# A gated cross-attention and feed-forward block in float32 on one core: a second x1 buffer, four ffn buffers, a reordered start and a reordered last tile

## What is computed

```
query = einsum('bnc,dc->bnd', ctx, Wq) + bq        # ctx: (4, 512, 256), d = 128
key   = einsum('bnc,dc->bnd', ctx, Wk) + bk
attention = softmax(einsum('bnd,bmd->bnm', query, key))
x = x + tanh(g_xattn) * einsum('bln,bmn->blm', layernorm(x), attention)
z = normalise(layernorm(x)) * ln_weight + ln_bias
x = x + tanh(g_ffn) * (einsum('bsk,ok->bso', z, sign(weight)) * max|weight| * gamma + beta)
```

## Time and profile before

| | us |
|---|---|
| median of 3 runs | 133.01 (132.58 to 133.08) |
| the profiled execution, its own time | 132.29 |
| its span, from the first to the last instruction | 130.8 |
| PE busy | 119.5 (91% of the span) |
| DVE busy | 94.8 (73%) |
| POOL busy | 92.3 (71%) |
| ACT busy | 86.8 (66%) |
| mean granted clock of PE | 0.977 of full |

### The profile page before, as it was taken

One profiled execution on the slowest core, in us unless ns is written; L12 is line 12 of the kernel. 1 busy time (PEld: TensorE's weight loads), 2 busy tenths in 40 slices (PEclk: granted clock), 3 DMA queues, 4 the chain that ended last, 5 costly groups with the idle time before them and its releaser, 6 DMA issues.

```text
span 130.8 us, 1869 instructions
## 1 busy us (share of the span) xinstructions
PE 119.5 (91%) x558; PEld 94.7 (72%) x558; DVE 94.8 (73%) x187; ACT 86.8 (66%) x185; POOL 92.3 (71%) x106
## 2 busy tenths in 40 slices
PE   5968999999999999948999999999999999999830
PEld 4517688888888878826888888878888888887730
DVE  1148699897988992479764992898859738997672
ACT  4243999999998889037797797179997940334300
POOL 3006899916329989998363799994649999839790
PEclk9999999999999999996899999999999999999996
DMA  3949999735532500247450502357000202220043
GB/s 80 246 141 393 392 388 296 306 76 152 186 89 74 160 0 5 83 147 250 165 160 0 160 0 85 116 205 228 13 3 3 74 11 80 80 80 0 0 182 139
DMA packets 10649, 17.15 MB, mean 131 GB/s; under 512 B 1808, under 2 KB 2576, under 8 KB 10640
## 3 DMA queue, kind: packets, MB, share of 16 engines
q1 hardware_dynamic: 9920, 17.04, 38.3%
q10 hardware_dynamic: 720, 0.00, 0.3%
HBM read 12.59 MB, written 4.19 MB: 128 GB/s over the span
## 4 chain that ended last, share of the span: by engine, by line
PE 53%; ACT 17%; POOL 14%; DVE 6%; issue 4%; POOLq 1%; ACTq 1%; DVEq 1%
PE ps_y L372 23%; PE ps_ffn L385 14%; POOL x L863 5%; PE ps_turn L339 4%; PE ps_score L332 4%; ACT prob L507 3%; PE ps_ffn L310 3%; POOL x L868 3%; PE ps_score L446 3%; ACT prob L513 2%; ACT k_hi L496 2%; POOL xt_lo L851 2%; ACT x_sb L544 2%; ACT q_hi L496 1%; DVE neg_max L640 1%
## 5 line engine op out<-in xcount | busy, mean ns | idle before, releaser
L863 POOL TENSOR_TENSOR x<-x,shift 128x512 f32<-128x512 f32 x16 | 21.1, 1320 | 8.1 <-ACT unread L538 8.1
L851 POOL TENSOR_TENSOR xt_lo<-xt_raw,xt_hi 128x512 fp32r<-128x512 f32 x16 | 21.6, 1350 | 7.3 <-ACT xt_hi L519 4.2
L685 DVE SCALAR_TENSOR_TENSOR zw<-x,neg_mean,ln_w 128x512 f32<-128x512 f32 x16 | 19.4, 1209 | 0.4
L868 POOL TENSOR_TENSOR x<-x,ffn 128x512 f32<-128x512 f32 x14 | 18.9, 1356 | 0.0
L372 PE MATMUL ps_y<-pt_hi,xt_hi 128*128 128x512 f32 x64 | 18.9, 418 | 0.0
L507 ACT ACTIVATE prob<-ps_score,neg_max 128x512 f32<-128x512 f32 x14 | 9.5, 681 | 13.8 <-DVE neg_max L640 13.8
L372 PE MATMUL ps_y<-pt_hi,xt_lo 128*128 128x512 f32 x64 | 18.4, 411 | 0.0
L555 ACT ACTIVATE zt_hi<-ps_turn 128x512 fp32r<-128x512 f32 x16 | 9.5, 594 | 12.9 <-PE ps_turn L339 12.9
L711 DVE SCALAR_TENSOR_TENSOR ffn<-ps_ffn,rstd,gain 128x512 f32<-128x512 f32 x15 | 11.2, 746 | 9.1 <-POOL x L868 4.1
L385 PE MATMUL ps_ffn<-w_sign,zt_hi 128*128 128x512 f32 x60 | 17.2, 408 | 0.5 <-DVE ffn L711 0.5
L372 PE MATMUL ps_y<-pt_lo,xt_hi 128*128 128x512 f32 x64 | 17.6, 396 | 0.0
(11 more groups left out here) (160 smaller groups left out, 241.5 us busy)
## 6 DMA issues: line engine op xcount, KB each, us to landing
xt_raw<-in_x_t_dram SPq DMA_DIRECT2D x16, 256.0 KB, 3.0
out_dram<-x SPq DMA_DIRECT2D x15, 256.0 KB, 2.0
ctx_sb<-in_ctx_t_dram SPq DMA_DIRECT2D x8, 256.0 KB, 6.8
x_sb<-in_x_dram SPq DMA_DIRECT2D x8, 256.0 KB, 5.0
ctx_sb<-in_x_dram SPq DMA_DIRECT2D x8, 256.0 KB, 6.2
w_raw<-in_weight_t_dram SPq DMA_DIRECT2D x4, 256.0 KB, 8.2
ln_w<-in_ln_weight_dram SPq DMA_DIRECT2D x1, 256.0 KB, 7.6
gain<-in_gamma_dram SPq DMA_DIRECT2D x1, 256.0 KB, 8.6
```

Source lines behind the costliest of these rows:

```text
L685: nc.vector.scalar_tensor_tensor(out=zw[:, t, :], in0=x1[:, t, :], scalar=neg_mean2[:, t:t + 1], in1=ln_w[:, :], op0=ALU.add, op1=ALU.mult)\
L851: nc.gpsimd.tensor_tensor(xt_lo[:, t, :, :], xt_raw[:, t, :, :], xt_hi[:, t, :, :].bitcast(f32), ALU.subtract).then_inc(xt_lo_done, 1)
L863: nc.gpsimd.tensor_tensor(x1[:, t, :], x1[:, t, :], shift[:, :], ALU.add).then_inc(x1b_done, 1)
L868: nc.gpsimd.tensor_tensor(x1[:, t, :], x1[:, t, :], ffn[:, t % 2, :], ALU.add)\
```

## The change

- `x1` gets a second buffer for the odd batches, in the place of the contexts of batches 2 and 3. `add_y` waits for a store only from batch 2 on, and then for that of two batches earlier.
- `ffn` has four buffers. `scale_ffn` waits for `add_ffn` of the same tile of the batch before.
- At the start the keys of batch 0 are projected first, then the queries in two halves of 256 columns, the second half into another bank (`ps_y[1]`); the first two `scores` need the first half alone. The query of batch 1 is projected with split operands, as all others were.
- The key weights are loaded by ACT's queue, ahead of the biases, and all three ahead of ACT's table load.
- On POOL `add_ffn(b, 0)` stands behind `power2(b, 1)` and `split_xt(b + 1, 1)`.
- In `last`, `power2(b, 0)` and `add_shift(b, 3)` stand earlier on POOL, the squares earlier on ACT, and DVE finishes each half of the last tile before it begins the other.
- On DVE two splits of batch 2's projection stand earlier.

The diff, cut to its core (declarations of semaphores and the places where only `x1` became `x1_buf[b % 2]` are left out):

```diff
-        ffn = sb("ffn", [P, 3, N])
+        ffn = sb("ffn", [P, T, N])
...
-        out_stored = [sem(f"out_stored{t}") for t in range(T)]
+        out_stored = [[sem(f"out_stored{i}_{t}") for t in range(T)] for i in range(2)]
...
+        x1_buf = (x1, ctx_sb[:, 2:4, :, :].rearrange("p b k l -> p (b k) l"))
...
+        q_first = ((ps_ffn[0], slice(0, L // 2), proj_ready), (ps_y[1], slice(L // 2, L), q_rest_ready))
...
-            for t in range(T):
-                sp.sem_inc(out_stored[t], 16)
+                sp.dma_start(out[b, t * P:(t + 1) * P, :], x1_buf[b % 2][:, t, :]).then_inc(out_stored[b % 2][t], 16)
+
+            load_ctx(0)
             sp.dma_start(wq_sb[:, :, :], wq_t.rearrange("(k p) d -> p k d", p=P)).then_inc(wq_in, 16)
-            load_ctx(0)
-            sp.dma_start(wk_sb[:, :, :], wk_t.rearrange("(k p) d -> p k d", p=P)).then_inc(wk_in, 16)
             load_ctx(1)
...
-                if b == 0 or (b, j) == (1, 0):
-
-                    for k in range(KC):
-                        if j == 0:
-                            pe.wait_ge(ctx_in[b][k], 16)
-                        mm = pe.matmul(bank[:, :], (wq_sb, wk_sb)[j][:, k, :], ctx_sb[:, b, k, :],
-                                       start=(k == 0), stop=(k == KC - 1))
-                    mm.then_inc(proj_ready, 1)
-                    return
...
+            def project_k0():
+
+                pe.wait_ge(wk_in, 16)
+                for k in range(KC):
+                    pe.wait_ge(ctx_in[0][k], 16)
+                    mm = pe.matmul(ps_ffn[1][:, :], wk_sb[:, k, :], ctx_sb[:, 0, k, :],
+                                   start=(k == 0), stop=(k == KC - 1))
+                mm.then_inc(proj_ready, 1)
+
+            def project_q0():
+
+                pe.wait_ge(wq_in, 16)
+                for bank, cols, ready in q_first:
+                    for k in range(KC):
+                        mm = pe.matmul(bank[:, cols], wq_sb[:, k, :], ctx_sb[:, 0, k, cols],
+                                       start=(k == 0), stop=(k == KC - 1))
+                    mm.then_inc(ready, 1)
+
             def scores(b, t):
+                if b == 0 and t == HALF:
+                    pe.wait_ge(q_rest_lo, 1)
                 if t == 0:
                     pe.wait_ge(proj_lo, 2 * (b + 1))
...
-            pe.wait_ge(wq_in, 16)
-            project(0, 0)
-            pe.wait_ge(wk_in, 16)
-            project(0, 1)
+            project_k0()
+            project_q0()
...
+            act.dma_start(wk_sb[:, :, :], wk_t.rearrange("(k p) d -> p k d", p=P)).then_inc(wk_in, 16)
+            act.dma_start(bqk[:, 1:2], bk.rearrange("(p a) -> p a", a=1)).then_inc(bias_in, 16)
+            act.dma_start(bqk[:, 0:1], bq.rearrange("(p a) -> p a", a=1)).then_inc(bias_in, 16)
             act.wait_ge(half_done, 1)
-
             nc.scalar.activation(table_in[:, :], neg_half[:, :], ACT.Tanh).then_inc(table_done, 1)
             act.wait_ge(table_done, 1)
-            act.dma_start(bqk[:, 0:1], bq.rearrange("(p a) -> p a", a=1)).then_inc(bias_in, 16)
-            act.dma_start(bqk[:, 1:2], bk.rearrange("(p a) -> p a", a=1)).then_inc(bias_in, 16)
...
-            for arrived, w, hi in ((wq_in, wq_sb, wq_hi), (wk_in, wk_sb, wk_hi)):
+            def round_k0():
+                act.wait_ge(proj_ready, 1)
+                nc.scalar.activation(k_hi[:, 0, :], ps_ffn[1][:, :], ACT.Identity,
+                                     bias=bqk[:, 1:2]).then_inc(proj_hi, 1)
+
+            def round_q0():
+                for (bank, cols, _), ready, count, done in zip(q_first, (proj_ready, q_rest_ready), (2, 1),
+                                                               (proj_hi, q_rest_hi)):
+                    act.wait_ge(ready, count)
+                    nc.scalar.activation(q_hi[:, 0, cols], bank[:, cols], ACT.Identity,
+                                         bias=bqk[:, 0:1]).then_inc(done, 1)
+
+            for arrived, w, hi in ((wk_in, wk_sb, wk_hi), (wq_in, wq_sb, wq_hi)):
                 act.wait_ge(arrived, 16)
                 nc.scalar.activation(hi[:, :, :], w[:, :, :], ACT.Copy).then_inc(w_hi_done, 1)
             act.wait_ge(bias_in, 16 * 2)
-            round_qk(0, 0)
-            round_qk(0, 1)
+            round_k0()
+            round_q0()
...
-            for t in range(T):
-                turned_ffn_hi(B - 1, t)
-                square_x1(B - 1, t)
+            square_x1(B - 1, 0)
+            square_x1(B - 1, 1)
+            turned_ffn_hi(B - 1, 0)
+            square_x1(B - 1, 2)
+            turned_ffn_hi(B - 1, 1)
+            square_x1(B - 1, 3)
+            turned_ffn_hi(B - 1, 2)
+            turned_ffn_hi(B - 1, 3)
...
-                dve.wait_ge(out_stored[t], 16 * (b + 1))
+                if b >= 2:
+                    dve.wait_ge(out_stored[b % 2][t], 16 * (b // 2))
                 dve.wait_ge(x_biased, T * b + t + 1)
                 dve.wait_ge(y_ready, T * b + t + 1)
-                nc.vector.scalar_tensor_tensor(out=x1[:, t, :], in0=ps_y[t % 2][:, :],
+                nc.vector.scalar_tensor_tensor(out=x1_buf[b % 2][:, t, :], in0=ps_y[t % 2][:, :],
...
-                if t >= 2:
-                    dve.wait_ge(out_done, T * b + t - 1)
-                nc.vector.scalar_tensor_tensor(out=ffn[:, t % 2, :], in0=ps_ffn[(t + 1) % 2][:, :],
+                if b > 0:
+                    dve.wait_ge(out_done, T * (b - 1) + t + 1)
+                nc.vector.scalar_tensor_tensor(out=ffn[:, t, :], in0=ps_ffn[(t + 1) % 2][:, :],
                                                scalar=rstd2[:, t:t + 1], in1=gain[:, :],
...
                 t = T - 1
+                dve.wait_ge(x1b_done, T * b + t + 1)
                 for h, cols in enumerate(halves):
                     dve.wait_ge(ffn_ready, 1 + T * b + t + 1 + h)
-                    nc.vector.scalar_tensor_tensor(out=ffn[:, 2, cols], in0=half_bank[h][:, cols],
+                    nc.vector.scalar_tensor_tensor(out=ffn[:, t, cols], in0=half_bank[h][:, cols],
                                                    scalar=rstd2[:, t:t + 1], in1=gain[:, cols],
                                                    op0=ALU.mult, op1=ALU.mult).then_inc(ffn_evac, 1)
-                dve.wait_ge(x1b_done, T * b + t + 1)
-                for h, cols in enumerate(halves):
                     dve.wait_ge(ffn_evac, 1 + T * b + t + 1 + h)
-                    nc.vector.tensor_tensor(x1[:, t, cols], x1[:, t, cols], ffn[:, 2, cols], ALU.add)\
+                    nc.vector.tensor_tensor(x1_buf[b % 2][:, t, cols], x1_buf[b % 2][:, t, cols], ffn[:, t, cols], ALU.add)\
                              .then_inc(last_out_done, 1)
...
-            for j, (w, hi, lo) in enumerate(((wq_sb, wq_hi, wq_lo), (wk_sb, wk_hi, wk_lo))):
+            for j, (w, hi, lo) in enumerate(((wk_sb, wk_hi, wk_lo), (wq_sb, wq_hi, wq_lo))):
                 dve.wait_ge(w_hi_done, j + 1)
                 nc.vector.tensor_tensor(lo[:, :, :], w[:, :, :], hi[:, :, :].bitcast(f32), ALU.subtract)\
                          .then_inc(w_lo_done, 1)
             dve.wait_ge(bias_in, 16 * 2)
-            rest_qk(0, 0)
-            rest_qk(0, 1)
+            dve.wait_ge(proj_hi, 1)
+            nc.vector.scalar_tensor_tensor(out=k_lo[:, 0, :], in0=ps_ffn[1][:, :], scalar=bqk[:, 1:2],
+                                           in1=k_hi[:, 0, :].bitcast(f32), op0=ALU.add, op1=ALU.subtract)\
+                     .then_inc(proj_lo, 1)
+            for (bank, cols, _), ready, count, done in zip(q_first, (proj_hi, q_rest_hi), (2, 1),
+                                                           (proj_lo, q_rest_lo)):
+                dve.wait_ge(ready, count)
+                nc.vector.scalar_tensor_tensor(out=q_lo[:, 0, cols], in0=bank[:, cols], scalar=bqk[:, 0:1],
+                                               in1=q_hi[:, 0, cols].bitcast(f32), op0=ALU.add,
+                                               op1=ALU.subtract).then_inc(done, 1)
...
+            rest_qk(2, 0)
             stats_x(0, (3,))
-            rest_qk(2, 0)
+            rest_qk(2, 1)
             weight_max(0)
-            rest_qk(2, 1)
...
-                add_ffn(b, 0)
                 power2(b, 1)
                 split_xt(b + 1, 1)
+                add_ffn(b, 0)
...
                 add_shift(b, 0)
+                power2(b, 0)
                 add_shift(b, 1)
-                power2(b, 0)
                 add_shift(b, 2)
                 power2(b, 1)
+                add_shift(b, 3)
                 add_ffn(b, 0)
                 add_ffn(b, 1)
-                add_shift(b, 3)
 
             nc.gpsimd.memset(neg_half[:, :], -0.5).then_inc(half_done, 1)
             nc.gpsimd.memset(q_hi[:, B - 1, :].bitcast(f32), 0.0).then_inc(later_zeroed, 1)
```

21 lines of the change are left out of this document (12 added, 9 removed).

## The result

| | before | after |
|---|---|---|
| median of the runs, us | 132.80 (132.05 to 133.08, 4 runs) | 124.38 (124.30 to 124.74, 4 runs) |
| ratio, 95% interval | | 0.938 (0.9335 to 0.9425) |
| profiled execution | 132.29 | 124.74 |
| its span | 130.8 | 122.8 |

Measured twice more, the same kernel took 125.12 us (124.95 to 125.35) and 124.78 us (124.09 to 125.55). So the runs shown first were on the lucky side, by about half a us (in their profile the clock came to full 1.1 us earlier than in the two later ones); even 125.12 lies just under the range, which ends at 125.2.

The account below looks back on a forecast made before the run. PE was taken to bound the steady state, ACT and PE the start, and short waits the end. Terms -0.5, -3.9 and -1.8 sum to -6.2 us: 126.1 profiled, 126.8 as median with 0.7 added; range 125.2 to 129.1.

Parts of the forecast that it names:

- The middle, -3.9: Batch 1's stretch on PE falls from 29.00 to 25.07 us: 2.3 of idleness and 1.6 of low clock.
- It costs nothing, its removal gives 0: DVE's 4.6 us of waits for stores, removed by the second `x1` buffer, were covered by PE's own work: 0.
- the moved `add_ffn` delays only a store, for which nothing waits: POOL's new order in batch 0's second half keeps the same sum of work and harms nothing.
- The rival in which the stall moves into batch 1: POOL's backlog makes `zw` or `xt_lo` late by up to 2 us; only the clock's 1.6 gained, 129.1 us; 16%.
- The clock's 1.6 us: Part of the middle's gain: PE's clock no longer falls to one half after its idleness for `zw`, 1.6 us.
- The start, -0.5: First stage: ACT's stream gains 0.25 us and PE 0.28 more; bounds 0 and -1.6.
- the hole closes: PE's 1.56 us of idleness for `k_lo` before the first `scores` goes, as keys are split during the queries' product.
- So ACT's stream of 27 us gains what the landing gains ... I take the middle, -0.25: ACT, without slack, gains only from contexts landing earlier, by one SP issue of half a us; 0.25 taken.
- The start comes whole: Rival: contexts land a us or more earlier and ACT's stream moves with PE's, 125.5 us; 10%.
- The end, -1.8: Behind PE's last feeds: last DVE addition at 126.5 instead of 128.26 us; bounds -0.9 and -2.3.
- The waits of 0.54 and 0.37: At the end, PE's wait for `scale_ffn` of tile 0 and the last additions' for `add_shift` of tile 3 go.
- 0.75 + 0.87 for tile 2: DVE's time for tile 2 at the end, within 3.5 us from PE's last full feed to the last addition.

Follow-up runs that it names:

- wk_sp_bias_late: Changed kernel with key weights back on SP's queue ahead of the contexts and biases back behind ACT's table load: 125.42 us, ratio to before 0.949.
- start_old: Changed kernel with its whole old start put back (loads, keys, queries, splits of batch 2): 126.49 us, kernel before 132.28.
- end_order: Changed kernel with the first half of the last tile scaled ahead of tile 2's addition on DVE: 123.94 us, run again 124.20.
- end_tile0: Changed kernel with the addition of the last batch's tile 0 on DVE instead of POOL: 125.04 us, kernel before 132.64.
- end_both: Changed kernel with the last tile's first half scaled ahead of tile 2's addition, and tile 0's addition moved to DVE: 125.49 us.
- ffn2: Changed kernel with two `ffn` buffers in batches 0 to 2, POOL's new order and two `x1` buffers kept: 127.37 us, kernel before 132.13.
- ffn2_pool_old: Changed kernel with two `ffn` buffers in batches 0 to 2 and POOL's old order, two `x1` buffers kept: 127.24 us, kernel before 131.33.
- x1_one: Changed kernel with a single `x1` buffer, four `ffn` buffers and POOL's new order kept: 127.07 us, kernel before 131.33.

## Why the prediction was right and wrong

**The middle, -3.9, was right in sum (4.04) and wrong in who earned it.** DVE's first wait (1.6 forecast, 1.65), the scaling of tile 3 behind `ffn_ready`, `zw` ahead of PE by about 1 us: all as worked out. Wrong was "It costs nothing, its removal gives 0", said of the second `x1` buffer, and "the moved `add_ffn` delays only a store, for which nothing waits". Nothing waits for it because of that buffer; without it DVE waits 3.71 us. The waits of the earlier trace rows were judged where they lay in the kernel before, behind a longer one, and not once that one was gone. POOL's new order, credited with part of the gain, gives nothing. The rival in which the stall moves into batch 1 didn't happen: POOL was busy 23.17 of 24.96 us there, and PE had no hole.

**The clock's 1.6 us is an amount for one profile.** Of the 38 runs of the kernel before that ran beside the experiments, 28 have a mean clock of 0.975 to 0.981, with a median of 132.50 us, and 10 one of 0.987 or more, with 131.40. Where their clock fell no trace shows; if it was there, the fall is worth near 0.8 us on the average run (28 of 38 times 1.1).

**The start, -0.5, is the step that failed; 1.90 was measured**, outside its bound of 1.6. In the two later profiles of the whole change it was 1.33 and 1.35, since the clock came to full an us later there than in the kernel before; at an equal rise it is 1.7 to 1.8. That the hole closes was right. The failed step is "So ACT's stream of 27 us gains what the landing gains ... I take the middle, -0.25". The landing gained 3.2 us and not a part of an issue slot, since the lull in the transfers went. ACT's stream then gained 1.3, nearly as much as PE's first `scores` (1.43), for its cast was no longer bound by the landing: it came at 11.42 and not a few tenths before 12.7. `wk_sp_bias_late` shows it: with the late landing the same computation gains 0.48. The rival "The start comes whole" describes what happened, and had 10% (its 1.3 us follows neither from the bound of 1.6 nor from the 2.0 on PE). Its one counterargument, "the landing times", was the quantity that the change moves. The Trainium skill, DMA: Bandwidth & Descriptors, section Issuing engines are not separate DMA queues, gave a sum that was too small as well, 6.5 instead of 6.2: that only the issue time is saved is not what these runs show, where moving one load took 1.1 to 2.8 us off SP's other issues.

**The end, -1.8, came as 1.53** and 0.41 behind the last addition. The waits of 0.54 and 0.37 went as forecast. "0.75 + 0.87 for tile 2" was mis-sized, 0.75 + 1.44, and so the last addition ended 3.96 us behind PE's last full feed and not 3.5. In the two later profiles the last part gained 1.78 and 1.80, with that addition at 1.18 and 1.17. That it meets the forecast is in part luck: DVE's part was 0.2 us longer than forecast, and PE's, from the last `scores` to its last full feed, gained 0.77 instead of 0.54.

The sum was 6.2 and the span gave 8.0: 1.4 us at the start, 0.14 in the middle, 0.12 in the last scores, 0.14 at the end and behind. The profiled time gained 7.55 of it, as 0.45 us more than before lies outside the span (1.94 against 1.49); `start_old` has 1.8 there too, so it isn't the start. So the profiled run came 1.36 us under the forecast's 126.1, out of the 2.42 us by which the median missed 126.8. The other 1.06 is no step of the mechanism: 0.7 was added since the profiled run of the kernel before lay that far under its median, and that of the changed kernel lay 0.36 above its own.

## What to carry to other kernels

Edits that look separate can be each other's price: ask of every delayed operation not only who waits for it now, but who would wait without the other edits. A resource without slack moves together with the input that feeds it, so before its slack is called the limit, ask whether the change moves that input. And before work is put into an engine's idle spell, look at what the neighbour does in that spell.

## What the runs showed of the hardware

**DVE's operations with two SBUF inputs, and POOL.** Four additions of 128x512 on DVE with both inputs in SBUF, begun while POOL ran one of its own, ended 0.55 to 0.56 us after POOL's ended: 118.97 after 118.42 (whole change), 119.26 after 118.70 (its run beside `end_order`), 116.28 after 115.72 (`end_tile0`), 116.86 after 116.31 (`end_both`). The one begun behind POOL's took 0.68. The scaling that reads PSUM took 0.75 with POOL active. That is a wait and not a slowdown. The Trainium skill, SBUF — State Buffer, section SBUF: two separate sides, says just this: the port pair that GpSimd and VectorE share is an exclusive lock, and a VectorE operation with two SBUF inputs that comes second to a GpSimd operation that reads SBUF is held until the other is done. The trace agrees, and the 1.44 us could have been forecast from it. The 0.87 that was used instead had been held too: it ended at 126.34, 0.55 us behind POOL's addition.

The same wait stood ahead of PE's hole in the kernel before. `centre` reads two rows of SBUF as well; where POOL did nothing beside it, it took 0.75 us (40 cases over all profiles). The one that PE waited for took 1.46 and ended 0.54 us behind POOL's addition, so by the timeline some 0.7 of the hole's 2.28 us are this wait, which no run takes out:

```profile
57.53 1.27 POOL L868 TENSOR_TENSOR x<-x,ffn 128x512 f32<-128x512 f32 x1
```

```profile
57.88 1.46 DVE L685 SCALAR_TENSOR_TENSOR zw<-x,neg_mean,ln_w 128x512 f32<-128x512 f32 x1
```

**A load's queue can cost more than its issue.** With 128 KB of key weights on SP's queue the transfers of 6.5 to 9.8 us ran at 138 to 174 GB/s (five profiles), with them on ACT's at 209 to 296 (fifteen).

**The same hole, another clock.** In the profiled run of the kernel before the clock fell behind a hole of 2.3 us on PE, and by their mean clock 28 of its 38 other runs seem to have had such a fall. In the twelve runs of `ffn2`, `ffn2_pool_old` and `x1_one`, whose profiles have the same hole, the mean clock was under 0.99 in two. What decides it stays open here.
